# The last doubling of a triangular inverse: 64x64 products that alternate between the two halves of the output partitions

## What is computed

```
def step(Sm, inp):
    q_, k_, v_, g_, b_ = inp
    Sm = Sm * jnp.exp(g_)[..., None, None]
    kv = jnp.einsum('bhk,bhkv->bhv', k_, Sm)
    delta = (v_ - kv) * b_[..., None]
    Sm = Sm + jnp.einsum('bhk,bhv->bhkv', k_, delta)
    o = jnp.einsum('bhk,bhkv->bhv', q_, Sm)
    return (Sm, o)
```

## Time and profile before

| what | value |
|---|---|
| median of three runs | 2876.7 us (2873.14 to 2880.99) |
| span of the profiled execution | 2973.8 us |
| TensorE busy in it | 2684.9 us, 90% |
| VectorE busy | 2384.7 us, 80% |
| ScalarE busy | 1828.3 us, 61% |
| GpSimd busy | 1221.2 us, 41% |
| mean granted TensorE clock | 0.954 of full speed |

### The profile page before, as it was taken

The page is one execution under the profiler, slowest core; times in us unless marked ns, Lnnn a source line. Parts: engine busy times, 40 slices in busy tenths (PEclk is TensorE's granted clock), DMA queues, the critical chain, the costliest instruction groups (busy, mean ns, idle before and its releaser), DMA issues. The chain is left out here.

```text
span 2973.8 us, 122804 instructions
## 1 busy us (share of the span) xinstructions
PE 2684.9 (90%) x52271; PEld 2275.1 (77%) x52272; DVE 2384.7 (80%) x5006; ACT 1828.3 (61%) x5749; POOL 1221.2 (41%) x1048
## 2 busy tenths in 40 slices
PE   1478889999999999999999999999999999857898
PEld 1367668888888888888888888888888888724555
DVE  7556658888888888888888888888888888468796
ACT  1245546777777777777777777777777777501111
POOL 2456555343434343434343434343434343255420
PEclk7778889999999999999999999999999999978999
DMA  5221101111111111111111111111111110152311
GB/s 189 92 61 42 32 23 38 35 42 35 42 35 42 35 42 35 42 36 41 39 42 41 39 39 42 41 40 37 42 35 42 35 32 28 61 192 90 94 64 43
DMA packets 92834, 153.27 MB, mean 52 GB/s; under 512 B 16966, under 2 KB 60661, under 8 KB 91107
## 3 DMA queue, kind: packets, MB, share of 16 engines
q1 hardware_dynamic: 69491, 111.65, 12.9%
q0 software_dynamic: 12288, 24.19, 2.6%
q10 hardware_dynamic: 10512, 9.57, 0.9%
HBM read 114.38 MB, written 40.37 MB: 52 GB/s over the span
## 5 line engine op out<-in xcount | busy, mean ns | idle before, releaser
L1383 DVE SCALAR_TENSOR_TENSOR p_y<-p_xr,cw,p_y 128x512 f32<-128x512 f32 x768 | 652.2, 851 | 66.7 <-ACT p_y L1101 46.6
L740 PE MATMUL p_psF<-xnS,w_hl 128*128 128x512 f32 x1536 | 432.8, 417 | 24.1 <-PEq L628 11.1
L1655 POOL TENSOR_TENSOR p_Wr<-p_Ws,p_rho 128x512 f32<-128x512 f32 x96 | 135.8, 1436 | 651.0 <-ACT p_Ws L1198 651.0
L740 PEld LDWEIGHTS p_psF<-xnS,w_hl 128*128 128x128 f32 x1536 | 279.3, 195 | 87.3 <-issue 18.2
L1637 POOL TENSOR_TENSOR p_E<-p_E,p_sj 128x512 f32<-128x512 f32 x128 | 158.0, 1253 | 292.9 <-DVE p_sj L1409 292.9
L800 PEld LDWEIGHTS p_psI<-p_Dc,p_M 32*32 32x32 f32 x16384 | 180.1, 106 | 100.0 <-issue 91.9
L922 PE MATMUL p_psO<-p_wout,p_ont 128*128 128x256 f32 x1024 | 250.4, 399 | 0.7 <-ACT p_ont L1211 0.7
L800 PE MATMUL p_psI<-p_Dc,p_M 32*32 32x32 f32 x16384 | 215.7, 195 | 38.1 <-issue 33.7
L1678 POOL TENSOR_TENSOR p_O<-p_OG,p_sm 128x512 f32<-128x512 f32 x128 | 131.4, 1049 | 240.9 <-DVE p_sm L58 240.8
L1098 ACT ACTIVATE p_xr<-p_psF 128x512 f32<-128x512 f32 x256 | 154.1, 602 | 123.0 <-PE p_psF L740 119.8
L810 PEld LDWEIGHTS p_psI<-p_Xs,p_DTc 32*32 32x32 f32 x16384 | 168.5, 106 | 75.0 <-issue 70.0
(11 more groups left out here) (322 smaller groups left out, 6638.8 us busy)
## 6 DMA issues: line engine op xcount, KB each, us to landing
p_ab<-decays SPq DMA_DIRECT2D x64, 512.0 KB
w_raw<-in_w_in SPq DMA_DIRECT2D x16, 768.0 KB, 5.6
p_wgu<-in_w_gu SPq DMA_DIRECT2D x60, 176.0 KB
expert_out<-p_ye ACTq DMA_DIRECT2D x73, 128.0 KB, 1.8
expert_in<-p_zero SPq DMA_DIRECT2D x16, 512.0 KB, 7.1
p_xe<-expert_in SPq DMA_DIRECT2D x60, 128.0 KB
p_wd<-in_w_down SPq DMA_DIRECT2D x60, 88.0 KB
p_wout<-in_w_out SPq DMA_DIRECT2D x16, 256.0 KB
```

The lines of the kernel that those rows point to most:

```text
L740: m = pe.matmul(b4(psF[f % 2][:, :]), w_hl[:, wp, kt, ty * P:(ty + 1) * P], xnS[:, xp, kt, :].rearrange("p (b t) -> p b t", b=B)[:, :, c * ...
L1383: m = dve.scalar_tensor_tensor(y[:, ty, :, :], xr[:, ty, :, tap:tap + P], cw[:, ty, tap:tap + 1], y[:, ty, :, :], ALU.mult, ALU.add)
```

## The change

The order of the eight products of `level6_x` and `level6_y` becomes sequence by sequence, the two value heads in turn, and the output partitions change with the head. In `level6_x` head 0 goes to partitions 64 to 127 and head 1 to 0 to 63, both in columns 0 to 255 of the bank; in `level6_y` head 0 goes to partitions 0 to 63 and head 1 to 64 to 127, both in columns 256 to 511. The operands stay where they were. As a head's results now lie on a half of their own, ScalarE copies them in two instructions of 64x256 and VectorE negates them in two of 64x256; the semaphore is raised by the second of each.

```diff
+        def side(v):
+            return slice(H * v, H * (v + 1))
...
                 for n in range(2 * B):
-                    v, b = n // B, n % B
-                    m = pe.matmul(psI[p][H:P, n * H:(n + 1) * H], ATP[p][0:H, v, b, 0, H:P], D64[:, v, b, :], start=True, stop=True)
+                    v, b = n % 2, n // 2
+                    m = pe.matmul(psI[p][side(1 - v), b * H:(b + 1) * H], ATP[p][0:H, v, b, 0, H:P], D64[:, v, b, :], start=True, stop=True)
...
                 for n in range(2 * B):
-                    v, b = n // B, n % B
-                    m = pe.matmul(psI[p][0:H, n * H:(n + 1) * H], Xs6[:, v, b, :], TT[p][H:P, v, b, H:P], start=True, stop=True)
+                    v, b = n % 2, n // 2
+                    m = pe.matmul(psI[p][side(v), 256 + b * H:256 + (b + 1) * H], Xs6[:, v, b, :], TT[p][H:P, v, b, H:P], start=True, stop=True)
...
                 if l < 6:
-                    src, dst = psI[p][:, 0:256], Xs[p][:, :, :, :].rearrange("p v b t -> p (v b t)")
+                    m = act.activation(Xs[p][:, :, :, :].rearrange("p v b t -> p (v b t)"), psI[p][:, 0:256], ACT.Copy)
                 else:
-                    src, dst = psI[p][H:P, :], Xs6.rearrange("p v b t -> p (v b t)")
-                act.activation(dst, src, ACT.Copy).then_inc(s["inverse_sb"], 1)
+                    for v in range(2):
+                        m = act.activation(Xs6[:, v, :, :].rearrange("p b t -> p (b t)"), psI[p][side(1 - v), 0:256], ACT.Copy)
+                m.then_inc(s["inverse_sb"], 1)
...
                 wait_event(dve, "inverse_mm", "y6", g)
-                dve.tensor_scalar(heads(TT[g % 2][0:H, :, :, H:P]), vb(psI[g % 2][0:H, :], H), -1.0, None, ALU.mult).then_inc(s["tt"], 1)
+                for v in range(2):
+                    m = dve.tensor_scalar(TT[g % 2][0:H, v, :, H:P], vb(psI[g % 2][side(v), 256:512], H), -1.0, None, ALU.mult)
+                m.then_inc(s["tt"], 1)
```

## The result

The changed kernel takes 2828.8 us (median of four runs, 2827.3 to 2831.8) against 2878.6 us for the kernel before in the same comparison: ratio 0.983, 95% interval 0.9815 to 0.9843, 49.8 us less. The prediction was 2826 us, 51 us less.

What follows compares the result with a forecast made beforehand. TensorE's queue was taken to bound the 57-step stretch: 0.93 us saved a step less some 0.03 is 0.9 us, x 57 = 51 us, taking the 2876.7 us median to 2826 us; range 2812 to 2862 us.

Steps and rivals of the forecast that it cites:

- What bounds the kernel: In the 57-step stretch TensorE's queue, 97.5% busy, sets the pace; a microsecond saved there shortens the step unless another engine follows closely.
- The overlap: level6_x and level6_y: one input strip feeds both column halves at once, saving 0.47 us a product, 0.93 us a step.
- Edits 2 and 3: ScalarE's level 6 copy and VectorE's level 6 negation, each split into two of 64x256: +0.1 us taken for each pair.
- The cover: ScalarE's copy ends 2.2 us before level6_y starts, so its longer pair costs nothing; without that cover, 0.1 us a step.
- What is next late: VectorE, from level 2's transpose to the second head's output, keeps about 0.1 us of the gain in the step examined.
- 0.94 us of waits: VectorE's waits in the examined step, 0.56 + 0.20 + 0.18 us, set against TensorE coming 0.93 us earlier.
- The seven steps counted at nothing: The steps outside the 57-step stretch, counted for 0; 6.5 us more if they gain in full.
- The profiled execution: It is 97 us longer than the 2876.7 us median; the 51 us gain is carried over in microseconds.
- No overlap: Rival: a 64-row strip does not feed two halves, products stay at 1.13 us, 2879 us; chance 0.12.
- A stop at each switch of the half: Rival: each column-half switch in a product costs 0.09 us; with no overlap 72 us lost, 2949 us; chance 0.07.
- Another engine takes half: Rival: ScalarE may be late in some steps, leaving about 0.45 us a step, 26 us, 2851 us; chance 0.11.

Runs made afterwards that it cites:

- x_twice: The changed kernel with level6_x's eight products run twice over, to the same place: 2859.6 us, ratio 0.9947.
- x_only: The changed kernel with level6_y and VectorE's single instruction as in the kernel before, so only level6_x alternates: 2850.5 us, ratio 0.9908.
- y_only: The changed kernel with level6_x and ScalarE's single copy as in the kernel before, so only level6_y alternates: 2854.1 us, ratio 0.9912.
- heads_first: The changed kernel's layout and copies, but all four products of head 0 first, then the four of head 1: 2862.1 us, ratio 0.9943.
- half_copied: The changed kernel without ScalarE's second 64x256 copy: 2828.7 us, ratio 0.9839.
- half_negated: The changed kernel without VectorE's second 64x256 negation: 2822.2 us, ratio 0.9815.
- after_again: The changed kernel itself, unaltered, measured again in a later comparison: 2827.8 us, ratio 0.9833.
- split_only: The kernel before with only ScalarE's copy and VectorE's negation each split into two of 64x256, products unchanged: 2876.0 us, ratio 1.0002.
- act_again: Second measurement of the changed kernel with the second head's negation on ScalarE instead of VectorE: 2817.9 us, ratio 0.9802.

## Why the prediction was right

**What bounds the kernel.** Right. x_twice gave TensorE 0.47 us a step and the steps grew by 0.45; x_only and y_only each gave about half.

**The overlap.** Right, with the predicted size: 0.46 us a product where 0.47 was taken, from lines 834 and 835, where one strip of 32 partitions fed two column groups. A round of two 64x64 records costs what a single one did, 0.058 us from start to start. Not tried was the alternation of the heads on one and the same half; in heads_first the records of one half still start 0.058 us apart. The rule of the Trainium skill (TensorE: Matmul & The Clock Gate, Part 3: Packing small matmuls) that weight loads overlap matmuls only where the row group differs would have left 1.13 us; the measured 0.68 us decides against it here.

**Edits 2 and 3.** Mis-sized: +0.1 us was taken for each pair and the upper ends came, 0.76 us against 0.59 on ScalarE and 0.84 against 0.68 on VectorE. The row to go by was the upper bound, two instructions end to end. The cover was rightly named for ScalarE (half_copied: no gain from leaving half away).

**What is next late.** The mechanism was right, its size not, and its place only in part. The prediction left 0.1 us behind VectorE in one kind of step of four, 0.03 on average. In truth 0.2 us of TensorE's 0.92 stayed behind on average, most in the first and the third chunk's steps, about 0.3 in each.

A first chunk's step was not worked out; there the larger average wait for level6_y was taken for slack. The trace of the kernel before had the sign against it: after that wait VectorE went on without another one to the decayed products, and TensorE waited for these (0.30 us at 1452.89). So the longer pair lies on the path there, as half_negated shows.

The third chunk's step was worked out, and its 0.94 us of waits are used up, in the step shown above with the wait for the decayed products after them. The pair took 0.16 us more and not 0.1, and the small addition beside GpSimd, a term that the prediction does not have, 0.84 us more. That this is what holds the step is not shown: the addition was short in 5 of 14 such steps of the changed kernel and in 3 of 14 of after_again, and these took 36.82 and 36.86 us, the others 36.95 and 36.84. What keeps the 0.3 us in this kind of step is open but for the 0.1 to 0.25 us that relieving VectorE gives back.

So the steps gave 0.71 us each and not 0.9, 40 of the 51 us. That the total came out near 51 owes something to what lies outside the 57 steps and to the spread of the runs: the spans of the two profiled executions compared above, 2873.2 and 2830.0 us, differ by 43 us, those of split_only and after_again (2826.1 us) by 47, the medians by 50. The seven steps counted at nothing and the tail can't be told from that spread.

**The profiled execution.** Carrying the gain over in microseconds was right: the execution profiled before took 100.6 us more than split_only's, of which the 57 steps have 1.5.

**The rivals.** No overlap: fell (0.68 us). A stop at each switch of the half: fell, the alternating records run at the old interval. Another engine takes half: its mechanism was there, on VectorE instead of ScalarE, and took at most a fifth (0.2 of 0.92 us, of which act_again got 0.15 back), not half.

## What to carry to other kernels

Small fp32 products that write to one half of the output partitions leave the other half of the array idle even when all operands sit on the same input partitions; alternate the output halves record by record, since TensorE looked ahead only about four records here. Count what the split result costs the engines that read it: two instructions on different partitions cost their full time each here, and the gain stays only where that engine has a wait to spare, or where the second half can go to an engine that has. Look for that wait in every kind of step, not in one, and look there for an engine that already waits for the one you are about to burden. Ask also what an engine that falls back by some tenths of a us will run into: here a small addition met GpSimd's product and took 1.0 us instead of 0.16.

## What was not expected of the hardware

TensorE started matmuls out of program order: in heads_first the second head's first record began while three of the first head's eight, ahead of it, had not. So the program order that is said of every engine's queue at the start does not hold strictly for TensorE's records. It fits that interleaving two and two kept most of the gain (0.73 against 0.68 us a product, 42 of 49 us).

Two copies in a row overlap on ScalarE when they read the same partitions (0.65 us for two of 0.373 in split_only, 0.09 us of overlap) and not when the second reads the other half (0.76 us for two of 0.378); VectorE shows the same, 0.75 for two of 0.411 against 0.84 for two of 0.420. The two kernels also differ in the columns that the second instruction reads and in whether it moves its data to the other partitions; which of these counts was not separated.

A small VectorE instruction met GpSimd: in the traces of the kernel before and of the changed kernel all 56 long additions of `key_scales` (1.00 us) started while GpSimd's product `p_Wr` ran and ended 0.02 to 0.03 us after it; none of the 72 short ones (0.16 us) started during one. Which of the two engines holds the other is not shown: GpSimd's product is longer then too (1.27 us in the step shown, 1.04 otherwise).
